# Retention layer and FP4 feed-forward on one core: all projection chunks written out, weight quantising spread over thirty chunks, values split at four other steps

## The reference

```python
def _L0_attn_ref(X, W_Q, W_K, W_V):
    D = GAMMA ** abs(n - m)                 # 0.9 ** distance
    Q = _xpos(X @ W_Q)                      # rotary embedding with a scale
    K = _xpos(X @ W_K, downscale=True)
    V = X @ W_V
    p_attn = softmax(Q @ K^T) * D
    return p_attn @ V

def _L0_ffn_ref(x, w_gate, w_up, w_down):   # fp4_linear: both sides to FP4 in blocks of 16
    h = silu(fp4_linear(x, w_gate)) * fp4_linear(x, w_up)
    return fp4_linear(h, w_down)

x = L0_attn_X
x = x + _L0_attn_ref(_layernorm(x), W_Q, W_K, W_V)
x = x + _L0_ffn_ref(_layernorm(x), w_gate, w_up, w_down)
```

## Time and profile before

| | us |
|---|---|
| median of 3 runs | 2710.19 (2708.26 to 2712.71) |
| the profiled execution, its own time | 2708.02 |
| its span in the trace | 2706.2 |
| PE busy | 2608.5 (96%) |
| DVE busy | 2179.9 (81%) |
| POOL busy | 1802.4 (67%) |
| ACT busy | 1519.2 (56%) |

### The profile page before, as it was taken

How to read it: one execution, slowest core, us unless ns; L and a number is a source line. 1 busy time by engine, 2 the same in 40 slices (tenths; PEclk the granted TensorE clock), 3 DMA queues, 4 the chain that set the end, 5 groups by cost and what they waited for, 6 DMA issues and landing times.

```text
span 2706.2 us, 52170 instructions
## 1 busy us (share of the span) xinstructions
PE 2608.5 (96%) x16418; PEld 2341.9 (87%) x16418; DVE 2179.9 (81%) x4841; ACT 1519.2 (56%) x2943; POOL 1802.4 (67%) x1692
## 2 busy tenths in 40 slices
PE   7998899999999999999999999999999999999996
PEld 6887779988899889988998899888998899889996
DVE  7999977777888788878877887778787878788875
ACT  6665455556555555555555555555556555565553
POOL 6989956666666666667666766666666766576664
PEclk9999999999999999999999999999999999999998
DMA  8776410012000300031002200120003100210000
GB/s 290 282 268 231 173 49 19 24 38 98 25 24 19 118 25 22 21 102 40 23 20 68 74 21 23 40 99 23 25 24 104 32 24 22 101 39 25 20 23 17
DMA packets 135881, 183.48 MB, mean 68 GB/s; under 512 B 10064, under 2 KB 93136, under 8 KB 135632
## 3 DMA queue, kind: packets, MB, share of 16 engines
q1 hardware_dynamic: 135632, 180.33, 19.5%
HBM read 102.69 MB, written 77.59 MB: 67 GB/s over the span
## 4 chain that ended last, share of the span: by engine, by line
PE 69%; POOL 8%; issue 4%; DVE 3%; ACT 2%; POOLq 0%; DVEq 0%; ACTq 0%
PE score L410 21%; PE acc L529 16%; PE ring L410 15%; PE acc L410 8%; PE ring L502 4%; PE ring L547 3%; POOL vals L834 2%; POOL probs L852 2%; POOL h_buf L873 2%; POOL hq_buf L877 1%; DVE smax L1063 1%; DVE xqT L1050 1%; PE ring L494 1%; ACT probs L697 1%; POOL xv L858 1%
## 5 line engine op out<-in xcount | busy, mean ns | idle before, releaser
L852 POOL TENSOR_TENSOR probs<-probs,decay 128x512 f32<-128x512 f32 (+3 forms) x432 | 526.3, 1235 | 454.2 <-ACT probs L697 454.2
L410 PE MATMUL score<-keys,q_st 128*128 128x512 f32 x3072 | 765.9, 399 | 2.6 <-ACT probs L697 1.9
L410 PEld LDWEIGHTS score<-keys,q_st 128*128 128x128 f32 x3072 | 561.9, 189 | 114.3 <-issue 2.1
L529 PE MATMUL acc<-vals,pT 128*128 128x256 f32 x4416 | 582.9, 283 | 10.0 <-DVE pT L1050 10.0
L529 PEld LDWEIGHTS acc<-vals,pT 128*128 128x128 f32 x4416 | 546.2, 189 | 23.8 <-issue 10.7
L410 PE MATMUL ring<-w_gu,xqT 128*128 128x512 f32 (+1 forms) x2304 | 510.2, 375 | 0.0
L1063 DVE TENSOR_REDUCE smax<-score 128x1 f32<-128x1024 f32 x256 | 313.2, 1224 | 235.6 <-PE score L410 234.9
L667 ACT ACTIVATE pT<-ring 128x512 fp32r<-128x512 f32 (+3 forms) x432 | 226.9, 535 | 442.5 <-PE ring L502 435.1
L410 PEld LDWEIGHTS ring<-w_gu,xqT 128*128 128x128 f32 x2304 | 418.8, 188 | 63.8
L858 POOL TENSOR_TENSOR xv<-xv,xe 128x256 f32<-128x256 f32 x128 | 94.5, 738 | 322.3 <-DVE xv L931 322.3
L1050 DVE TENSOR_TENSOR pT<-ring,pT 128x512 fp32r<-128x512 f32 (+3 forms) x432 | 250.9, 605 | 70.7 <-ACT pT L667 70.6
(11 more groups left out here) (122 smaller groups left out, 4120.2 us busy)
## 6 DMA issues: line engine op xcount, KB each, us to landing
k_dram<-keys SPq DMA_DIRECT2D x56, 512.0 KB, 4.3
keys<-k_dram SPq DMA_DIRECT2D x56, 512.0 KB, 7.4
q_raw<-q_dram SPq DMA_DIRECT2D x129, 128.0 KB, 2.6
x_in<-X SPq DMA_DIRECT2D x32, 512.0 KB, 4.1
q_dram<-q_stage SPq DMA_DIRECT2D x32, 512.0 KB, 5.2
x_res<-X SPq DMA_DIRECT2D x128, 128.0 KB, 2.0
out<-x_res SPq DMA_DIRECT2D x128, 128.0 KB, 1.7
v_dram<-v_stage SPq DMA_DIRECT2D x28, 512.0 KB, 2.9
```

What stands on the lines that cost most here:

```text
L410: mm = pe.matmul(dst, stat(a, k), mov(m, k), start=i == 0, stop=i == n - 1)
L529: mm = pe.matmul(pv_out, pT[g % 2][:, a, j * P:(j + 1) * P], vals[m][:, kb, :], start=i == 0, stop=i == n - 1)
L852: pool.tensor_tensor(probs[:, k0 * P:k1 * P], probs[:, k0 * P:k1 * P], decay[:, off:off + (k1 - k0) * P], ALU.mult).then_inc(decayed, 1)
```

## The change

- **Loops.** `LOOPED` is gone: PE, ACT, POOL and DVE (and SP) have all 32 chunks written out.
- **Weights.** `weights` starts at chunk 2 and takes ten chunks a matrix (`W_FROM, W_CHUNKS = 2, 10`). DVE does one of six parts in each of the first six; POOL does its subtraction and its multiplication in halves, one in each of the last four. SP loads each matrix behind the spill of chunk 0, 10 and 20 instead of all three at the start.
- **Rotation.** The products with cos are one instruction of 1024 columns, the product with sin is negated, and POOL's adds become one instruction of 1024 columns for the keys and one for the queries.
- **Layer norm.** `mv1` gets a third column that holds EPS, and variance plus EPS is a TENSOR_REDUCE over two columns instead of a TENSOR_SCALAR.
- **Start.** DVE prepares only W_K, then normalises chunk 0 itself in one pass (`normalised_first`); W_Q and W_V follow after `chunk_x(0, 0)`. PE waits for each weight where it needs it.
- **Attention.** `V_SPLIT = (T - 3, 0, 1, 4)`: value chunk 0 of the next batch is split at step 13 of this one (in the last batch too, where it is a reload of batch 1), chunks 1, 2 and 3 at steps 0, 1 and 4. PE waits once for both halves of the exponentials, ahead of score column block 0, instead of once for each half.

```diff
-LOOPED = B // 2
-W_PARTS = 4
+W_FROM, W_CHUNKS = 2, 10
+V_SPLIT = (T - 3, 0, 1, 4)
...
+        def values_at(at, s):
+            return [c for c in range(NC) if s == V_SPLIT[c] and (c == 0 or at[2] is loop_plan)]
...
+                    if (i * NC + c) % W_CHUNKS == 0 and i * NC + c < 3 * W_CHUNKS:
+                        chunk_weight((i * NC + c) // W_CHUNKS)
...
+                if s == V_SPLIT[0] - 3:
+                    load_values(j + 1, 0, not is_first, more)
...
-                    elif o % 2 == 0:
-                        pe.wait_ge(exped, 2 * g - 1 + o // 2)
+                    elif o == 0:
+                        pe.wait_ge(exped, 2 * g)
...
-                pool.tensor_tensor(rot_k[c % 2][:, 0, :], rot_k[c % 2][:, 0, :], rot_k[c % 2][:, 1, :], ALU.subtract)
-                pool.tensor_tensor(rot_k[c % 2][:, 2, :], rot_k[c % 2][:, 2, :], rot_k[c % 2][:, 3, :], ALU.add).then_inc(rot_added, 1)
+                pool.tensor_tensor(rot_k[c % 2][:, 0:2, :], rot_k[c % 2][:, 0:2, :], rot_k[c % 2][:, 2:4, :], ALU.add).then_inc(rot_added, 1)
...
-                n, part = divmod(u - W_PARTS, W_PARTS)
-                if 0 <= n < 3 and part == 0:
+                n, part = divmod(u - W_FROM, W_CHUNKS)
+                h, part = part % 2, part // 2
+                half, few = slice(h * WC // 2, (h + 1) * WC // 2), slice(h * WB // 2, (h + 1) * WB // 2)
+                if 0 <= n < 3 and part == 3:
                     pool.wait_ge(w_rounded, n + 1)
-                    pool.tensor_tensor(w_stage[n], w_stage[n], w_exp, ALU.subtract).then_inc(w_levelled, 1)
+                    pool.tensor_tensor(w_stage[n][:, half], w_stage[n][:, half], w_exp[:, half], ALU.subtract).then_inc(w_levelled, 1)
...
-                for c in ((0, 1), (2,), (3,))[s] if at[2] is loop_plan and s < 3 else ():
+                for c in values_at(at, s):
                     values(at, c)
...
-                dve.tensor_scalar(var1[c % 2][:], mv1[c % 2][:, :, 1], EPS, None, ALU.add).then_inc(ln1_var, 1)
+                dve.tensor_reduce(var1[c % 2][:], mv1[c % 2][:, :, 1:3], AX.X, ALU.add).then_inc(ln1_var, 1)
...
-                dve.tensor_tensor(buf[:, 0, :], even, cos, ALU.mult)
-                dve.tensor_tensor(buf[:, 1, :], odd, sin, ALU.mult)
-                dve.tensor_tensor(buf[:, 2, :], odd, cos, ALU.mult)
+                dve.tensor_tensor(buf[:, 0:2, :], score[:, 2 * h:2 * h + 2, :], cos.unsqueeze(1).to_broadcast([P, 2, CH]), ALU.mult)
+                dve.scalar_tensor_tensor(buf[:, 2, :], odd, -1.0, sin, ALU.mult, ALU.mult)
                 dve.tensor_tensor(buf[:, 3, :], even, sin, ALU.mult).then_inc(rotated, 1)
...
+            def normalised_first():
+                dve.wait_ge(ln1_rstd, 1)
+                dve.tensor_scalar(minus_rstd[:], rstd1[0][:], -1.0, None, ALU.mult).then_inc(centred, 1)
+                dve.wait_ge(centred, 1)
+                for t in range(CT):
+                    op = dve.tensor_scalar(x_in[0][:, t, :], x_in[0][:, t, :], mv1[0][:, t, 0:1], minus_rstd[:, t:t + 1], ALU.subtract, ALU.mult)
+                op.then_inc(xn_ready, 1)
...
+            normalise(0, 0)
+            projection_weights(0)
+            normalised_first()
             normalise(0, 1)
             chunk_x(0, 0)
+            projection_weights(1)
+            projection_weights(2)
```

More of the change, by code:

```diff
@@ L331, in chunks @@
                     spill(i, b, c, following)
-            with nc.Fori(0, B - 2, engines=bass.OrderedEngineSet([sp.engine]), hint_back_edge=True) as i:
-                chunks(i, i + 1, i + 2)
-            chunks(B - 2, B - 1, 0)
+                    if i * NC + c == 0:
+                        chunk_tab(3)
+                    if (i * NC + c) % W_CHUNKS == 0 and i * NC + c < 3 * W_CHUNKS:
+                        chunk_weight((i * NC + c) // W_CHUNKS)
+            for i in range(B - 1):
+                chunks(i, i + 1, (i + 2) % B)
             for c in range(NC):
@@ L372, in step @@
                         load_keys(j, c)
+                if s == V_SPLIT[0] - 3:
+                    load_values(j + 1, 0, not is_first, more)
                 if s == T - 2 and more:
-                    for c in range(2):
-                        load_values(j + 1, c, not is_first)
-                if s < 2 and not is_first:
-                    load_values(j, s + 2)
+                    load_values(j + 1, 1, not is_first)
+                if s in (0, V_SPLIT[1] + 1) and not is_first:
+                    load_values(j, 3 if s else 2)
                 if s >= XR or not is_first:
@@ L444, in _ @@
             pe.wait_ge(ident_in, 16)
-            pe.wait_ge(wqkv_lo, 6)
             chunk_x(0, 0)
-            with nc.Fori(0, LOOPED, engines=bass.OrderedEngineSet([pe.engine]), hint_back_edge=True) as i:
-                for c in range(NC):
-                    chunk(i, c, ahead(i, c, 1))
-            for i in range(LOOPED, B):
+            for i in range(B):
                 for c in range(NC):
@@ L617, in chunk_k @@
                 act.wait_ge(rot_added, 2 * (i * NC + c) + 1)
-                act.activation(keys[0][:, :, c * CH:(c + 1) * CH], rot_k[c % 2][:, 0:4:2, :], ACT.Copy).then_inc(k_hi, 1)
+                act.activation(keys[0][:, :, c * CH:(c + 1) * CH], rot_k[c % 2][:, 0:2, :], ACT.Copy).then_inc(k_hi, 1)
             def chunk_v(i, c):
@@ L650, in queries @@
                 act.activation(q_st[s % 2][:, 0, :, :], q_raw[s % 2][:], ACT.Copy).then_inc(q_hi, 1)
-            normalised(0, 0)
             chunk_x(0, 0)
             normalised(0, 1)
-            with nc.Fori(0, LOOPED, engines=bass.OrderedEngineSet([act.engine]), hint_back_edge=True) as i:
-                for c in range(NC):
-                    chunk(i, c)
-            for i in range(LOOPED, B):
+            for i in range(B):
                 for c in range(NC):
@@ L815, in _ @@
                 rstd_chunk(0, c)
-            with nc.Fori(0, LOOPED, engines=bass.OrderedEngineSet([pool.engine]), hint_back_edge=True) as i:
-                for c in range(NC):
-                    chunk(i, c)
-            for i in range(LOOPED, B):
+            for i in range(B):
                 for c in range(NC):
@@ L989, in weights @@
             def weights(u):
-                n, part = divmod(u, W_PARTS)
-                if n >= 3 or part >= 4:
+                n, part = divmod(u - W_FROM, W_CHUNKS)
+                if not 0 <= n < 3 or part > 5:
                     return
-                then, wait, count = chain(w_step, n * NSTEP_W + (0, 3, 4, 6)[part])
+                then, wait, count = chain(w_step, n * NSTEP_W + (0, 1, 3, 4, 5, 6)[part])
+                wait()
                 if part == 0:
@@ L1022, in chunk, with projection_weights @@
                     kept_v(c)
-            normalise(0, 0)
-            wqkv = (1, 0, 2)
-            for i in wqkv:
+            for x in mv1:
+                dve.memset(x[:, :, 2], EPS).then_inc(eps_set, 1)
+            dve.wait_ge(eps_set, 2)
+            def projection_weights(order):
+                i = (1, 0, 2)[order]
                 dve.wait_ge(wqkv_in[i], 16)
```

67 lines of the change are left out of this document (33 added, 34 removed).

## The result

| | before | after |
|---|---|---|
| median in us | 2710.81 (2708.26 to 2712.71), 4 runs | 2678.3 (2672.07 to 2681.48), 4 runs |
| ratio, 95% interval | | 0.9877 (0.986 to 0.9894) |
| the profiled execution, its own time | 2708.02 | 2681.48 |
| its span | 2706.2 | 2679.4 |

The kernel is 32.5 us faster by the medians, 1.2%. The profiled execution is the slowest of the four after, so its span has only 26.8 us less.

What follows compares the result with a forecast made beforehand. PE was taken to bound the projection's looped half and nearly all of attention, DVE the projection's other half. The terms 27 + 2 - 2 + 13 = 40 us off 2708.0 gave 2668, forecast as 2670 (2655 to 2680; wider range 2650 to 2690).

Steps and rivals of the forecast that it cites:

- 27 us are won: Projection: of 32.2 us that PE loses to other engines in 30 chunks, 27 are won by PE keeping 9.24 a chunk.
- 5 us: Projection: the part of the 32.2 us lost to other engines that stays, from POOL's lag (bounds none and 14).
- about 1 us of PE for each of the first two matrices: Projection: PE's loss to POOL running up to 3.3 us behind late in a matrix, with 2.7 free.
- 0.66 at best before: DVE's variance in the projection: its best time as TENSOR_SCALAR, against 0.2 us expected as a reduction.
- The wide products: Rotation: the wide cos product saves DVE one start, 0.05 us; POOL's two wide adds take the split's 2.36 each.
- The halves on POOL and their loads: Projection weights: two halves of 1.6 and two of 1.3 us a matrix; loads cost 0 to 1 us each.
- 2.2 us: Start: DVE normalises chunk 0 in instructions of 0.3 us, PE starts at about 10.2; 2.2 us won (bounds 1 and 3).
- -2 us: Into attention: 1.1 us lost waiting for both halves of the exponentials, 1 us to POOL's later last key split.
- 13 us: Attention: waits 2.4 instead of 4.36 us, 1.95 won at seven places, less 0.5 for the reload (bounds -4 and 24).
- Writing the first 16 chunks out: Projection: PE already keeps 9.28 us a chunk across the loop's back edges, so nothing is won: 0.
- POOL takes over: Rival, projection: 15 or so DVE weight instructions each pay 1 us more beside POOL; about 14 us gone, 2684; chance 0.17.
- Attention wins nothing: Rival, attention: the stalls only move to steps 13 and 4, giving 2683 us; chance 0.12.

## Why the prediction was right, and where not

The time came 8 us above the 2670 forecast. That is inside the range of 2655 to 2680 behind the sum and inside the 2650 to 2690 that the prediction names further on. The case was the forecast's own: PE carries the pace in both stages. Of the 40 us summed, 26.8 stand in the profiled execution, and 2.3 of these lie behind the last store, where the sum had nothing. One of the prediction's own signs of being wrong did appear, DVE rows of over 2 us beside POOL's adds. By its steps:

- **"27 us are won" in the projection:** 23.05 in the first trace, 27.9 in the second of the same kernel (281.5 us against the 309.4 of before). The mechanism was right: the 27 ordinary chunks at 9.24, the clock at 0.99, the variance at 0.16 us in all chunks, no chunk late behind the subtraction. The term of what stays, "5 us", measured 9.2 and 4.3. What I had inside it was wrong in kind: I spread 1 us over each matrix for POOL's lag, and it came as one instruction of 5.3 us, up to twice a run. The estimate that POOL falls up to 3.3 us behind was fair: in chunk 14 the variance is there at 140.64 and POOL's `rstd` begins at 143.68, 3.0 later. The weakest step is "about 1 us of PE for each of the first two matrices", and with it "each of the 15 or so then pays some 1 us more" as the price of meeting POOL in the rival. Most pay nothing, and one or two pay for three POOL instructions. "0.66 at best before" for the variance was misread: five of the 32 rows take 0.17 us. Of the edits behind the 23 us only the reduction was run alone and the wide forms were undone; the spreading over thirty chunks was not, nor the written-out loops, so their shares are argued from the traces.
- **The wide products:** 1.23 us for the wide one against two of 0.68, which start 0.60 apart: 0.05 won each, as taken. On POOL 2.4 to 2.5 us against 2.36 taken from the split. Undoing them costs 12 us, more than any row of before shows.
- **The halves on POOL and their loads:** 1.71 and 1.40 us (1.6 and 1.3 forecast). All waits of DVE for x together are 2.7 us in the projection, and nothing on PE hangs on them.
- **"2.2 us" at the start:** 1.6. PE's transposes begin at 10.47, not 10.2; DVE's four passes take 1.38 us instead of 1.2, and 0.4 of the gain is gone by the second chunk's transposes.
- **"-2 us" into attention:** -3.9. The exponentials' wait is 3.03 against 1.93, the 1.1 forecast. POOL's last key split costs 2.56 where 0.65 stood before, 1.9 and not 1; the remaining 0.9 I put down to the lower clock behind the two waits.
- **"13 us" in attention:** 3.6 to the last store. The waits came out at 0.22, 1.09 and 1.40 behind steps 13, 0 and 1 (forecast 0.5, 0.4, 1.4, and 0.15 at step 4): 1.65 won a batch against 1.95. The miss at step 0 is the 1.09, which goes when the value chunk is split behind `hq_buf`. The split alone won 12.0 us and so confirms this term. What the sum lacked altogether is a term for the layout: 1.1 us a batch in matmuls that wait for nothing, because two small tiles grew and one is new. With 32 bytes of padding a batch takes 289.0, 1.7 less than before, 12 us over seven.
- **"Writing the first 16 chunks out: 0":** the first 14 chunks take 9.23 to 9.44 us in the first trace and 9.23 to 9.31 in the second, so the written-out code costs next to nothing, as the loop's back edges did not.

The rival "POOL takes over" had the right place (the weight instructions beside POOL's adds) and less than its price: 9.2 and 4.3 us of the 32.2 stayed in the two traces, where it needed 19. "Attention wins nothing" came mostly true, by the layout; its own reason, stalls that move to steps 13 and 4, did not hold: they are 0.22 us and none.

## What to carry to other kernels

A rewritten form on DVE is worth what its neighbours let it be worth: take one shut-out instruction away and the next of its kind is shut out, as long as POOL lags. Look for the stretch in which POOL is never idle, and put there only what does not wait for it, or give POOL less to do. When an edit adds or widens a small tile, pad until the later tiles stand where they stood or 128 bytes further on, as here, before timing it, or the layout's part is read as the edit's. And work put last in a step pays only if the consumer of that step doesn't want it first.

## What the runs showed of the hardware

- A DVE instruction of 88 columns (0.20 us alone) that begins beside a POOL instruction can be held over several that follow each other without a gap: 5.3 to 5.4 us to the end of the third, 5.6 and 5.9 us to the end of the fourth where they are narrow, 6.9 us over three with a wide subtraction among them. TENSOR_SCALAR and SCALAR_TENSOR_TENSOR, both with all operands in SBUF, behave alike; TENSOR_REDUCE and the products from PSUM ran through at their usual 0.16 and 0.68 us beside a busy POOL.
- It is not always so: the variance of the kernel before (four columns, 0.17 us alone) took 0.6 to 0.9 us in 23 of 32 chunks, to the end of one POOL instruction, with the next one right behind. The scales were held when they began 0.49 us or more before the end of a 1024-column add and got in (0.19 to 0.41 us) when they began 0.35 us or less before it; what decides was not tried.
- PE matmuls of 256 columns with `vals` and `pT` stand 118.3 ns apart in the mean with most tiles 96 bytes behind their old places, and 116.4 and 115.7 with them at the old places and 128 bytes behind; the 96 bytes cost 1.1 us in 290 and, in the kernel before, 10 us in all.
- The same 12 matmuls behind the same wait of 1.9 us took 3.03 us in one run (granted clock 1.00) and 5.46 in another (0.50, which is 1.2 GHz): whether the clock is down behind a short wait varies by run.
